# A decoder layer on one core: layer-norm transposes, q, k and v of the cross-attention in another PSUM bank, x loaded in place, another step order

## The reference

```
x = x + attn(layernorm(x))                 # causal, 8 heads of 128, one shared k and v head
x = x + xattn(layernorm(x), ctx)           # 16 heads of 16; adds a (256,256) mask and a
                                           # (16,256,256) bias per batch, twice; softmax; Wo, bo
x = x + ffn(layernorm(x))                  # shared expert + top 2 of 8: w2 @ relu(w1 @ x)^2,
                                           # weighted by sigmoid gates, normalised over the two
```

## Time and profile before

| | us |
|---|---|
| median of 3 runs | 2559.81 |
| the profiled execution | 2559.14 |
| its span, first to last instruction | 2557.4 |
| PE busy | 2340.5 (92%) |
| ACT busy | 2060.2 (81%) |
| DVE busy | 2007.8 (79%) |
| POOL busy | 1788.1 (70%) |
| mean granted TensorE clock | 0.991 of full speed |

### The profile page before, as it was taken

How to read it: one execution, slowest core, us unless ns; L and a number is a source line. 1 busy time by engine, 2 the same in 40 slices (tenths; PEclk the granted TensorE clock), 3 DMA queues, 4 the chain that set the end, 5 groups by cost and what they waited for, 6 DMA issues and landing times.

```text
span 2557.4 us, 77106 instructions
## 1 busy us (share of the span) xinstructions
PE 2340.5 (92%) x26176; PEld 2036.7 (80%) x26176; DVE 2007.8 (79%) x6672; ACT 2060.2 (81%) x6065; POOL 1788.1 (70%) x1899
## 2 busy tenths in 40 slices
...
GB/s 167 92 105 87 92 86 89 84 109 86 92 88 89 84 109 82 96 87 90 84 109 81 96 86 91 85 109 80 94 87 93 84 109 80 93 88 93 80 100 10
DMA packets 171126, 233.14 MB, mean 91 GB/s; under 512 B 20720, under 2 KB 119280, under 8 KB 170736
## 3 DMA queue, kind: packets, MB, share of 16 engines
...
## 4 chain that ended last, share of the span: by engine, by line
PE 63%; DVE 13%; ACT 11%; issue 10%; POOL 3%; DMA 1%; SPq 0%; DVEq 0%; ACTq 0%; POOLq 0%
PE ps_c_out L955 10%; PE ps_c_hidden L955 10%; PE ps_a_misc L955 9%; PE ps_b_probsT L1083 8%; PE ps_b_misc L1097 3%; PE ps_b_misc L955 3%; PE ps_b_scores L1071 3%; PE ps_a_scores L1009 3%; PE ps_a_misc L1028 2%; DVE b_neg_scores L817 2%; POOL bias L510 2%; DVE a_qT L769 2%; PE ps_b_probsT L955 2%; PE ps_b_scores L955 2%; PE ps_a_probsT L1016 1%
## 5 line engine op out<-in xcount | busy, mean ns | idle before, releaser
L510 POOL TENSOR_TENSOR bias<-bias,b_mask 128x512 f32<-128x512 f32 x512 | 646.9, 1278 | 0.0
L817 DVE CUSTOM_DVE_ANT_0 b_neg_scores<-ps_b_scores,bias 128x256 f32<-128x256 f32 x1024 | 391.7, 419 | 95.3 <-PE ps_b_scores L1071 34.8
L531 POOL TENSOR_TENSOR c_hidden_lo<-c_hidden,c_hidden_hi 128x512 f16<-128x512 f32 x288 | 334.2, 1160 | 131.2 <-ACT c_hidden_hi L683 90.8
L825 DVE TENSOR_TENSOR b_probsT_lo<-ps_b_probsT,b_probsT_hi 128x512 f16<-128x512 f32 x512 | 352.7, 689 | 63.6 <-ACT b_probsT_hi L660 53.7
L1083 PE MATMUL ps_b_probsT<-constants,b_probs 128*128 128x128 f32 x2048 | 323.3, 281 | 29.1 <-DVE b_probsT_lo L825 15.1
L524 POOL TENSOR_TENSOR c_hidden<-c_relu 128x512 f32<-128x512 f32 x288 | 300.3, 1043 | 56.3 <-ACT c_relu L678 55.2
L660 ACT ACTIVATE b_probsT_hi<-ps_b_probsT 128x512 f16<-128x512 f32 x512 | 303.1, 592 | 24.8 <-PE ps_b_probsT L1083 20.0
L955 PE MATMUL ps_c_out<-w_hi,c_hidden_hi 128*128 128x256 f16 x1152 | 314.3, 273 | 5.0 <-DVE acc L926 2.7
L955 PE MATMUL ps_c_hidden<-c_xT_hi,w_hi 128*128 128x256 f16 x1152 | 314.6, 273 | 3.7 <-ACT c_relu L678 2.3
L955 PE MATMUL ps_c_hidden<-c_xT_hi,w_lo 128*128 128x256 f16 x1152 | 314.8, 273 | 0.0
L955 PE MATMUL ps_c_hidden<-c_xT_lo,w_hi 128*128 128x256 f16 x1152 | 314.7, 273 | 0.0
...
## 6 DMA issues: line engine op xcount, KB each, us to landing
bias<-in_bias SPq DMA_DIRECT2D x256, 512.0 KB, 3.5
q_stack<-qk_scratch SPq DMA_DIRECT2D x256, 64.0 KB, 2.4
...
k_stack_even<-qk_scratch SPq DMA_DIRECT2D x128, 64.0 KB, 2.4
k_stack_odd<-qk_scratch SPq DMA_DIRECT2D x128, 64.0 KB, 2.4
```

Source lines behind the costliest of these rows:

```text
L510: gp.tensor_tensor(part, part, b_mask[:, :], ALU.add).then_inc(b_c_ok, 1)
L531: gp.tensor_tensor(c_hl[:, u, :], c_h[:, :], c_hh[:, u, :], ALU.subtract).then_inc(c_h_ok, 1)
L817: last = dve.tensor_tensor_reduce(out=b_t[:, u, c, :], in0=ps_bs[:, c * T:(c + 1) * T], in1=bias[:, slot, at:at + T], scale=-2.0, scalar=3 ...
L825: dve.tensor_tensor(b_pTl[:, j % 2, :, :], ps_bpt[:, :].rearrange("p (c t) -> p c t", c=CT), b_pTh[:, j % 2, :, :], ALU.subtract).then_inc ...
```

## The change

- `b_T`, `b_q`, `b_kv` of stage b write to `ps_c_hidden`. In PE's order they stand behind `c_f1:8` of an earlier batch and ahead of `c_T` and `c_f1:0` of the next one; `b_kv` is cut into part 0 (k) and part 1 (v), each with a wait for the one before it in the bank.
- SP loads x into `x1`, after `x1` of the batch before has been used; `a_wo` adds in place. `x_res` is gone.
- The five tables are new, and the largest distance between batches of entries is 5 iterations instead of 3.

No instruction of an engine is added or taken away; each keeps its form and size.

```diff
-        b_pv:15@2 a_pt:7@1 a_pv:6@1 b_o:0@2 c_f2:8@3 a_pv:7@1 b_wo:0@2 a_wo:0@1 c_T:0@2 b_kv:0@1 a_T:0@0
+        b_s:11@2 c_f1:6@3 b_pt:8@2 c_f2:4@3 b_pv:7@2 b_s:12@2 a_wo:0@1 c_f1:7@3 a_T:0@0 c_f2:5@3 b_s:13@2
...
-LAGS = 3
+LAGS = 5
...
-        ln_bank = {"a": ps_am, "b": ps_bm, "c": ps_c1}
+        ln_bank = {"a": ps_am, "b": ps_c1, "c": ps_c1}
...
-                sp.wait_ge(x1_ok, after(b, 1, 0))
-                sp.dma_start(x_res[:, :, :], x_d[b]).then_inc(s_xres, 16)
+                sp.wait_ge(b_res_ok, after(b, 1, 0))
+                sp.wait_ge(s_xn["b"], after(b, 2, 0))
+                sp.dma_start(x1[:, :, :], x_d[b]).then_inc(s_xres, 16)
...
-                dve.wait_ge(b_res_ok, after(b, 1, 0))
                 dve.scalar_tensor_tensor(out=x1[:, :, :], in0=ps_am[:, :].rearrange("p (c d) -> p c d", c=CT),
-                                         scalar=1.0 / W_UP, in1=x_res[:, :, :], op0=ALU.mult,
+                                         scalar=1.0 / W_UP, in1=x1[:, :, :], op0=ALU.mult,
...
+                    if st == "a":
+                        pe.wait_ge(x1_ok, b)
+                    elif st == "b":
+                        pe.wait_ge(c_r_ok, max(NX * (b - 1), 0))
+                    else:
+                        pe.wait_ge(c_r_ok, NX * b)
+                        pe.wait_ge(b_vf_ok, min(b + 2, BATCHES))
...
+                if part == 0:
+                    pe.wait_ge(b_qf_ok, CD * (b + 1))
...
+                else:
+                    pe.wait_ge(b_kf_ok, CD * (b + 1))
...
             def b_s(b, j):
                 if j == 0:
                     pe.wait_ge(b_qst_ok, after(b, STACK, STACK))
                     pe.wait_ge(b_kst_ok, after(b, STACK, STACK))
-                    pe.wait_ge(b_vf_ok, after(b, 1, 1))
...
             def b_pv(b, j):
                 if j == 0:
-                    pe.wait_ge(b_qf_ok, after(b, 2, 2))
+                    pe.wait_ge(x2_ok, after(b, 1, 0))
```

118 lines of the change are left out of this document (57 added, 61 removed).

## The result

The changed kernel takes **2622.22 us** (median of 4 runs, 2621.31 to 2622.93), the kernel before on the same chip 2559.31 us: a ratio of **1.0244 [1.0226, 1.0262]**, slower. The forecast was 2568 us with a range to 2615, so the direction was the likeliest case's and the size was not. The profiled execution of the changed kernel has a span of 2619.5 us at a mean granted clock of 0.966; before it was 2557.4 us at 0.991.

The account below looks back on a forecast made before the run. PE was taken as the bound, waiting mostly for DVE. Per batch - 3.5 - 3.0 + 7.0 = + 0.5 us, + 16 us over 31 periods, - 8 for start and end: 2568 us from 2559.1, range 2490 to 2615.

Parts of the forecast that it names:

- the likeliest case: Whole kernel: the forecast of 2568 us, 0.3% slower; chance 0.46 for 2552 to 2600 us.
- Large waits go: PE's three large waits for DVE at the scores of stages a and b vanish: gain 3.5 us per batch.
- Small gaps: Some twenty small PE gaps, 4.7 us per batch: 1.7 us stays, so gain 3.0 us.
- c_T, 2.75: At c_T, less PE work covers the 5.1 us chain from b_wo, so c_f1:0 starts 2.75 us late per batch.
- Masks ahead of b_s:7: DVE's list up to the scores of head 7, gate parts 0 to 6 included, makes b_s:8 2.5 us late.
- g_sum and g_weights: Both stand ahead of b_pt:5's lo part on DVE; b_pt:6 and c_f2:2 wait 1.75 us in all.
- The three together: Losses at c_T, b_s:8 and b_pt:6 with c_f2:2: 7.0 us per batch, bounds 3.0 and 8.5.
- second count: From b_n to b_pt:7's lo part, DVE has 35 us of work, PE 32: at least 3 us lost.
- Start and end: First gate logits near 171 us, + 20; the end gains 31 or 20; together - 8 us, bounds - 25 and + 15.
- Moves of SP: The k stack's DMAs, x into x1 and late bias loads cost nothing; b_s:0 has 3 us of cover.
- late-stack rival: At b_s:0 the k stack comes late, 2 us lost per batch: 2630 us; chance 0.10.
- faster rival: Gate parts 4 to 6 and 10 to 12 cost less if POOL is idle then: 2510 us; chance 0.36.

Follow-up runs that it names:

- masks_later: The changed kernel with gate part 6 (the two g_mask) moved on DVE from ahead of b_s:7's scores to behind b_s:8's; 2531.95 us, ratio 0.9895.
- order_alone: The changed kernel, whole gate, with g_mask behind b_s:8, g_weights behind b_pt:5's low part on DVE, c_f2:2 behind c_f1:5 on PE; 2479.75 us, ratio 0.9689.
- busy_pe: The changed kernel with the six matmuls of a_pv:6 issued four times, same result, just ahead of b_pt:6; 2577.00 us, ratio 1.0071.
- own_buffer: The changed kernel with x loaded into its own buffer x_res again, with the old waits, instead of into x1; 2620.81 us, ratio 1.0241.

## Why the prediction was wrong

- **Large waits go, 3.5.** Right: the longest wait at the scores of a is 0.3 us, not 1.5. The 0.98 us wait at a scores of b just ahead of c_T belongs to the next term.
- **Small gaps, 1.7 left of 4.7.** Too careful: about 0.6 us is left in the period from 1276.08, outside the three stalls and the slow matmuls.
- **c_T, 2.75.** The size was right (measured 2.56), the place not. c_f1:0 does not start late behind one wait over 1 us at c_T; five gaps from 1346 to 1351 (1.15, 0.42, 0.30, 0.45, 0.24 with their hidden tails) make 2.56 us. DVE is late a step earlier. (In most periods the first of them is 0.2 us less and the wait at b_s:8 0.1 to 0.2 us more, with the same sum.)
- **Masks ahead of b_s:7, 2.5.** Measured 1.85 (1.69 visible and the tail), right in place and cause.
- **g_sum and g_weights, 1.75.** Measured 2.28 at b_pt:6 and 0.35 at c_f2:2, 2.6 in all: both g_weights were held for a whole POOL instruction here (1.99 us, against 1.30 in the earlier trace rows).
- The three together: 7.04 us, forecast 7.0. The forecast's second count beside them, DVE's 35 us of work against PE's 32 in the heavy stretch, was the wrong reason: masks_later and order_alone leave DVE all its instructions, and first one stall goes, then both. Part of those 35 us was time held by POOL, 1.7 us at the masks alone.
- **The step that failed: the clock, which is no term of the sum.** 68.6 + 7.0 + 1.7 was to be 77.3 us. The period from 1276.08 has 69.2 us of matmuls (68.8 in the kernel before by the same count), 7.0 of stalls, 0.6 of other gaps and 1.6 of slow matmuls: 78.4, and lasts 78.33. I priced each stall by its length alone and took PE's 0.109 us as fixed. The kernel before was read at 1.00 in its steady part, with no stall above 1.7 us, and whether a new pair of 1.9 and 2.3 us might lower the clock was not asked. busy_pe gets the 1.6 us back, and the periods are then 76.81, the same as before (76.84). So without the dips the new order would have about drawn level: the stalls alone cost what the large waits and the small gaps gave back.
- **Start and end, - 8.** Measured 26.3 - 11.5 - 0.4 = + 14.4, the other large miss. The start is 6 us of it, and all of these are there at the first b_s: it stands at 105.92, 13 us behind the earlier trace rows and not 7, after a wait of 2.26 us that the trace puts down to issue. The last of the 16 stack DMAs, one of the k stack, lands at 105.83; by the trace this is what b_s:0 waited for. The next batch's a_T waits 5.6 us for ACT's x_ln. At the end the last period is 61.4 us, not under 55: c_T of the last batch waits 4.93 us for c_xn, as in the earlier trace rows, and the period before it (74.3) has the heavy stretch's stalls still. So the end was better than the kernel before by 12 us, where I had 20 to 31.

```profile
105.92 0.37 PE L1078 MATMUL ps_b_scores<-k_stack_even,q_stack 128*128 128x256 f16 x1 [2.26 <-issue]
...
2583.51 0.94 PE L982 MATMUL ps_c_hidden<-constants,c_xn 128*128 128x128 f32 x4 [4.93 <-ACT c_xn L564]
```

- **Moves of SP, nothing.** Right for the steady part: no wait of PE for a stack or a DMA is among its waits, and own_buffer excludes the x load. The late-stack rival is out there, and that its 2630 us lies near 2622 is chance. But the cover was less than the 3 us forecast: from batch 2 to 30 the last stack lands 0.9 to 2.3 us ahead of b_s:0, and for batches 0, 1 and 31 only 0.1 us ahead of it, so there b_s:0 may have waited for it. POOL waited 12.3 us in all for bias loads, in three waits; what they cost no run shows.
- **The faster rival** named the right lever (whether POOL is idle under the gate parts) and the wrong outcome for this kernel: parts 5, 6, 8 and 12 all met POOL at work. With one step moved the time comes near its price: masks_later is 22 us above the 2510 I gave it, by another sum (one stall and most of the dips).

In sum: 62.1 us = 47.7 (29 periods) + 14.4. Forecast were 14.5 for these 29 periods (0.5 each; 16 for all 31) and - 8 for start and end. Of the 33 us missed in the periods, the dips (1.67 us a batch by busy_pe, 48 us) are more than all; the other terms took 15 back: the small gaps are 1.1 us a batch shorter than the 1.7 I had left, the count of matmuls 0.6 us longer. Of start and end I can say where they wait, but no run undoes it, so that the cause is told by the trace alone.
